# Ten graph steps and an attention layer on one core: dense groups finished one by one, node features in two copies, two VectorE operands moved to PSUM

## What is computed

```python
# part 1: ten steps over all edges and self loops
wn = w * inv_sqrt_out[s] * inv_sqrt_in[d]
def step(h, _):
    agg = segment_sum(h[s] * wn[:, None], d, num_segments=n)
    return (1.0 - ALPHA) * agg + ALPHA * feat_0
x = layernorm(x + ten_steps(x))
# part 2: edge attention, 8 heads of 8
score = Kh[src] * Qh[dst] * inv_sqrt_d * Eh            # Eh = edge_attr @ WE + bE
score = exp(clip(score.sum(-1), -5, 5))
wV = segment_sum(Vh[src] * score, dst, num_segments=n)
x = layernorm(x + wV)
```

## Time and profile before

| | |
|---|---|
| median of 3 runs | 13,851.04 us (13,825.7 to 13,856.41) |
| the profiled execution | 13,848.15 us, its span 13,846.3 us |
| busy | PE 73%, PEld 41%, DVE 41%, ACT 5%, POOL 64% |
| mean granted TensorE clock | 0.762 |
| DMA | 3,491.10 MB, mean 252 GB/s |

### The profile page before, as it was taken

How to read it: one execution, slowest core, us unless ns; L and a number is a source line. 1 busy time by engine, 2 the same in 40 slices (tenths; PEclk the granted TensorE clock), 3 DMA queues, 4 the chain that set the end, 5 groups by cost and what they waited for, 6 DMA issues and landing times.

```text
span 13846.3 us, 141202 instructions
## 1 busy us (share of the span) xinstructions
PE 10055.4 (73%) x48612; PEld 5626.1 (41%) x48612; DVE 5672.0 (41%) x18837; ACT 688.7 (5%) x2111; POOL 8874.1 (64%) x8640
## 2 busy tenths in 40 slices
PE   0199994877868778688686886867868676777667
PEld 0199991332323323233232332333323355555555
DVE  6188881342333333333333333332333434444444
ACT  0033330000000000000000000000000010000000
POOL 3678887666666666666666666666666646666555
PEclk5555556988979889799797997989979855555555
DMA  9963335988969879699696996979969643333333
GB/s 394 385 165 69 69 54 174 374 296 310 375 228 374 328 273 375 227 375 363 236 376 231 373 374 225 373 265 336 377 228 374 249 110 108 113 109 110 106 105 97
DMA packets 1722567, 3491.10 MB, mean 252 GB/s; under 512 B 820288, under 2 KB 836067, under 8 KB 1721846
## 3 DMA queue, kind: packets, MB, share of 16 engines
q1 hardware_dynamic: 1145060, 2896.46, 56.9%
q0 software_dynamic: 379456, 296.48, 9.9%
q10 hardware_dynamic: 197330, 289.05, 5.8%
HBM read 3177.87 MB, written 303.14 MB: 251 GB/s over the span
## 4 chain that ended last, share of the span: by engine, by line
PE 55%; issue 15%; DVE 14%; another core or an unknown queue 8%; ACTq 5%; POOL 1%; ACT 1%; DMA 1%; DVEq 0%; SPq 0%
PE banks L1977 39%; PE banks L1996 5%; ACTq L1495 5%; PE banks L1946 4%; DVE arena L1673 2%; DVE arena L1737 2%; PE banks L1947 2%; PE banks L2067 1%; PE banks L2043 1%; DVE arena L1851 1%; PE banks L1989 1%; POOL dense L1460 1%; ACT arena L1504 1%; DVE arena L1687 1%
## 5 line engine op out<-in xcount | busy, mean ns | idle before, releaser
L1471 POOL DMA_INDIRECT arena<-node_rows,src_idx x5880 | 5623.7, 956 | 3174.3 <-issue 1655.0
L1977 PE MATMUL banks<-arena,u_sb 128*64 128x512 f32 x19600 | 5680.6, 625 | 1481.9 <-issue 1248.3
L1977 PEld LDWEIGHTS banks<-arena,u_sb 128*64 128x64 f32 x19600 | 1765.4, 142 | 4722.1 <-issue 4699.1
L1752 DVE TENSOR_TENSOR arena<-banks,arena 128x104 f32<-128x104 f32 (+20 forms) x1030 | 259.5, 257 | 5356.9 <-remote 4728.4
L1486 POOL DMA_INDIRECT arena<-kv_rows,src_idx x1568 | 1581.8, 1009 | 1136.8 <-DVEq L1910 553.0
L1737 DVE TENSOR_SCALAR arena<-banks,rel,w_tab 128x128 f32<-128x128 f32 x5880 | 1963.5, 403 | 166.5 <-issue 100.5
L1460 POOL DMA_INDIRECT dense<-arena x980 | 1633.5, 1667 | 591.9 <-issue 246.6
L1946 PE MATMUL banks<-arena 128*128 128x98 f32 x3136 | 1140.8, 467 | 694.8 <-ACT arena L1504 694.8
L1996 PE MATMUL banks<-arena 128*64 128x128 f32 x11760 | 1039.2, 301 | 661.6 <-issue 425.7
L1996 PEld LDWEIGHTS banks<-arena 128*64 128x64 f32 x11760 | 794.3, 149 | 925.0 <-issue 721.3
L1946 PEld LDWEIGHTS banks<-arena 128*128 128x128 f32 x3136 | 848.9, 331 | 702.9 <-ACT arena L1504 702.8
(11 more groups left out here) (166 smaller groups left out, 5382.1 us busy)
## 6 DMA issues: line engine op xcount, KB each, us to landing
arena<-dense SPq DMA_DIRECT2D x4900, 512.0 KB
dense<-blank ACTq DMA_DIRECT2D x5, 50176.0 KB, 371.2
arena<-in_dst_dram SPq DMA_DIRECT2D x195, 512.0 KB
arena<-node_rows,src_idx POOLq DMA_INDIRECT x5880
arena<-in_edge_attr_dram SPq DMA_DIRECT2D x195, 256.0 KB
u_sb<-key_rows SPq DMA_DIRECT2D x25, 1280.0 KB
u_sb<-in_edge_weight_dram SPq DMA_DIRECT2D x25, 1280.0 KB
arena<-key_rows SPq DMA_DIRECT2D x24, 1280.0 KB
```

Source lines behind the costliest of these rows:

```text
L1471: gp.indirect_dma_start(out=rows_in[:, n % ROWS, s, :], out_offset=None, in_=node_rows[k % 2], in_offset=bass.IndirectOffsetOnAxis(ap=src_ ...
L1977: last = mm(banks[h * D:(h + 1) * D, g, :], u_sb[:, j * D:(j + 1) * D], ring[:, u % SLOTS, h * 512:(h + 1) * 512], start=m < GROUPS, stop= ...
```

## The change

Five things change together.

- The dense columns shrink from 5,120 to 4,992 (39 blocks): the last group has 896 columns, in the matrix, its clear, its loads and its matmuls.
- The units run group by group (`UNIT`): all 98 blocks for group 0, then group 1. They spread over 96 iterations. A group ends one iteration after its last unit, at 20, 39, 58, 77 and 96. Two PSUM banks take turns as accumulators.
- A step reads the features from one copy and writes the new ones to the other (`u_of`). The second copy takes 6,272 elements per partition: the ring falls from 18 to 15 slots and the gather buffers from 7 to 6.
- GpSimd waits for all of its adds to land before the steps.
- In the attention, the bases of the picks are copied into PSUM bank 7 for 24 iterations at a time (9 small copies), and ScalarE writes the exponentials into that bank. `pick` and the message product then have one operand in SBUF.

```diff
-DENSE_COLS = 5120
+DENSE_COLS = 4992
-SLOTS = 18
-ROWS = 7
-DENSE_ITERS = 84
+SLOTS = 15
+ROWS = 6
+DENSE_ITERS = 96
...
-    GROUP_AT = {DENSE_ITERS + 2 * g: g for g in range(GROUPS)}
+    LAST_BLOCKS = list(GROUP_BLOCKS[-1])
+    BLOCK_AT = [b for b in range(NB) if b not in LAST_BLOCKS] + LAST_BLOCKS
+    UNIT = [(g, j) for g in range(GROUPS) for j in BLOCK_AT]
     UNIT_AT = [n * DENSE_ITERS // UNITS for n in range(UNITS)]
-    BLOCK_AT = [(i + DENSE_BLOCKS) % NB for i in range(NB)]
+    GROUP_AT = {UNIT_AT[(g + 1) * NB - 1] + 1: g for g in range(GROUPS)}
...
-                if i >= DENSE_ITERS and not copied:
-                    act.wait_ge(unit_used, (k + 1) * UNITS)
-                    for g in range(GROUPS):
-                        nc.scalar.activation(dense_sum[:, g, :], banks[:, g, :], ACT.Copy).then_inc(sum_copied, 1)
-                    copied = True
+                for turn, g in GROUP_AT.items():
+                    if turn <= i and g == copied:
+                        nth = k * GROUPS + g
+                        act.wait_ge(unit_used, k * UNITS + (g + 1) * NB)
+                        if nth >= 2:
+                            act.wait_ge(sum_turned, nth - 1)
+                        nc.scalar.activation(dense_sum[:, nth % 2, :], banks[:, nth % 2, :], ACT.Copy).then_inc(sum_copied, 1)
+                        copied += 1
...
+        for s in range(STREAMS):
+            pool.wait_ge(added[s], 16 * ROUNDS)
...
-            return v.tensor_tensor(u3, part, o3, ALU.mult)
+            return v.tensor_tensor(new3, part, o3, ALU.mult)
...
-                nc.scalar.activation(score[:, a % 2, :, :], score[:, a % 2, :, :], ACT.Exp).then_inc(exp_made, 1)
+                nc.scalar.activation(exp_ps(a), score[:, a % 2, :, :], ACT.Exp).then_inc(exp_made, 1)
...
-            v.tensor_tensor(pick[:, a % 2, :].rearrange("p (t e) -> p t e", e=P), att_buf(a).rearrange("p (t e) -> p t e", e=P), base_p[:, t].unsqueeze(2).broadcast_to([P, 8, P]), ALU.is_equal).then_inc(pick_made, 1)
+            at = P + 4 * (a % (2 * BASE_TURNS))
+            if a % BASE_TURNS == 0:
+                upto = min(PAIRS, 4 * (a + BASE_TURNS))
+                edge(v.tensor_copy(banks[:, 7, at:at + upto - 4 * a], base_p[:, 4 * a:upto]))
+            base_ps = banks[:, 7, at:at + 4]
+            v.tensor_tensor(pick[:, a % 2, :].rearrange("p (r e) -> p r e", r=4), att_buf(a).rearrange("p (r e) -> p r e", r=4), base_ps.unsqueeze(2).broadcast_to([P, 4, 2 * P]), ALU.is_equal).then_inc(pick_made, 1)
```

More of the change, by code:

```diff
@@ L51 @@
 KV_BUFS = 4
+BASE_TURNS = 24
 ARENA = 29696
@@ L1048, in __init__ @@
         self.blank_set = sem("blank_set")
-        self.dense_cleared = [sem(f"dense_cleared{g}") for g in range(DENSE_COLS // GROUP)]
+        self.dense_cleared = [sem(f"dense_cleared{g}") for g in range(-(-DENSE_COLS // GROUP))]
         self.flag_ready = sem("flag_ready")
@@ L1080, in fast @@
     assert BASE[DENSE_TILES // 2 - 1] + P <= DENSE_COLS
-    GROUPS = DENSE_COLS // GROUP
+    GROUPS = -(-DENSE_COLS // GROUP)
+    WIDTH = [min(GROUP, DENSE_COLS - g * GROUP) for g in range(GROUPS)]
     ITERS = (TILES - DENSE_TILES) // TPI
@@ L1085, in fast @@
     DENSE_BLOCKS = DENSE_COLS // P
+    assert DENSE_BLOCKS * P == DENSE_COLS and WIDTH[-1] > 512
+    GROUP_BLOCKS = [range(8 * g, min(8 * g + 8, DENSE_BLOCKS)) for g in range(GROUPS)]
     FIRST_BLOCK = BASE[DENSE_TILES // 2] // P
     LATE = DENSE_BLOCKS - FIRST_BLOCK
+    assert GROUP_BLOCKS[-1][0] <= FIRST_BLOCK < DENSE_BLOCKS
     assert ITERS * TPI == TILES - DENSE_TILES and ITERS % 2 == 0 and DENSE_TILES % 2 == 0
@@ L1317, in fast @@
     for n, (kind, i, what) in enumerate(UPDATES):
-        for b in (what if kind == "tail" else range(what * 8, what * 8 + 8)):
+        for b in (what if kind == "tail" else GROUP_BLOCKS[what]):
             UPDATED_AT[b] = n
-            last_use = max(UNIT_AT[m] for m in range(UNITS) if BLOCK_AT[m // GROUPS] == b)
-            assert last_use <= i - (kind == "dense")
     assert len(UPDATED_AT) == NB
@@ L1474, in run_pool @@
         pool.wait_ge(steps_done, 1)
-        base_v = base_p.rearrange("p (r u) -> p r u", u=2)
         for at, n, first, slope in RUNS:
-            last = pool.iota(base_v[:, at:at + n, :], pattern=[[slope, n], [0, 2]], base=first, channel_multiplier=1, allow_small_or_imprecise_dtypes=True)
+            last = pool.iota(base_p[:, at:at + n], pattern=[[slope, n]], base=first, channel_multiplier=1, allow_small_or_imprecise_dtypes=True)
         last.then_inc(att_tables, 1)
@@ L1524, in run_act @@
                 act.wait_ge(updated, k * len(UPDATES) + n + 1)
-                j0, m = (what * 8, 8) if kind == "dense" else (what[0], len(what))
-                act.dma_start(to[j0 * P:(j0 + m) * P, :].rearrange("(j p) f -> p j f", p=P), u_sb[:, j0 * D:(j0 + m) * D].rearrange("p (j f) -> p j f", f=D)).then_inc(node_stored, 16)
+                blocks = GROUP_BLOCKS[what] if kind == "dense" else what
+                j0, m = blocks[0], len(blocks)
+                act.dma_start(to[j0 * P:(j0 + m) * P, :].rearrange("(j p) f -> p j f", p=P), u_new[:, j0 * D:(j0 + m) * D].rearrange("p (j f) -> p j f", f=D)).then_inc(node_stored, 16)
         kvq_at = 0
@@ L1757, in run_dve, with update @@
         step = Chain(dve, step_vec, fin.n)
-        def update(part, j0, m):
-            u3 = by_node(u_sb, j0, j0 + m)
+        def update(k, part, j0, m):
+            u3, new3 = by_node(u_of[k % 2], j0, j0 + m), by_node(u_of[(k + 1) % 2], j0, j0 + m)
             x3 = by_node(x_sb, j0, j0 + m)
@@ L1788, in run_dve @@
                     if len(late) < len(done):
-                        last = update(parts[:, len(late):len(done), :], done[len(late)], len(done) - len(late))
+                        last = update(k, parts[:, len(late):len(done), :], done[len(late)], len(done) - len(late))
                         last.then_inc(updated, 1)
@@ L1797, in run_dve @@
                     dve.wait_ge(sum_turned, k * GROUPS + g + 1)
-                    part = banks[:, g, :].rearrange("p (j f) -> p j f", f=D)
-                    if g * 8 + 8 > FIRST_BLOCK:
-                        b0 = FIRST_BLOCK - g * 8
-                        assert 0 <= b0 < 8 and g == GROUPS - 1
-                        step(v.tensor_tensor(part[:, b0:8, :], part[:, b0:8, :], carry[:, :, :], ALU.add))
-                    last = update(part, g * 8, 8)
+                    j0, m = GROUP_BLOCKS[g][0], len(GROUP_BLOCKS[g])
+                    part = banks[:, (k * GROUPS + g) % 2, 0:m * D].rearrange("p (j f) -> p j f", f=D)
+                    if g == GROUPS - 1:
+                        step(v.tensor_tensor(part[:, FIRST_BLOCK - j0:m, :], part[:, FIRST_BLOCK - j0:m, :], carry[:, :, :], ALU.add))
+                    last = update(k, part, j0, m)
                     last.then_inc(updated, 1)
-                    dve.wait_ge(updated, k * len(UPDATES) + UPDATED_AT[g * 8] + 1)
+                    dve.wait_ge(updated, k * len(UPDATES) + UPDATED_AT[j0] + 1)
                     dve.sem_inc(sum_read, 1)
```

43 lines of the change are left out of this document (25 added, 18 removed).

## The result

After takes 14,097.8 us (median of 4, 14,091.1 to 14,115.3), before 13,848.7 (4, 13,825.7 to 13,856.4): 1.0185 of before, 95% interval 1.0172 to 1.0198. That is 249 us slower, inside the range; the point, 13,866, was not it.

A forecast was written before the change was run, and what follows sets the result against it. Gathers and hand-offs, not DMA bandwidth, were taken to bound a step. From 13,848 us, steps +20 and +40, adds' landing +3, copies +2, attention -50, median +3 gave 13,866 us; range 13,620 to 14,150.

The forecast's parts named there:

- What bounds a step: In the steps, gathers and hand-offs between engines, not DMA bandwidth, set the pace: 8.77 us per window in two-window runs.
- The steps' terms, +20 and +40: Over ten steps: +20 us for a longer stream of gathers, +40 us for each step's last windows and closing.
- The hand-offs inside the stretch: Four group hand-offs per step among the units: taken as 0, with 31 us a step if TensorE's cover is gone.
- The DMA share: Sign in the steps' stretch: the share falls to about 0.87, from 0.99, if the forecast is right.
- The rival of transfers (8%): Transfers bound the steps' stretch: a step takes 806 us instead of 883, the kernel near 13,100 us; chance 8%.
- The attention, -50 with bounds of 0 and 82: Attention gathers lose 52 ns each with one pick operand in PSUM: 50 us saved, between 0 and 82.
- the rival "turn into gaps": The attention's delays stay or turn into gaps: +50 us, 13,916, within the forecast's own range; no separate chance given.
- The sum: Whole kernel: 13,848 + 20 + 40 + 3 + 2 - 50 = 13,863 us, and 3 more for the median: 13,866.
- the third rival: TensorE falls behind in the steps: four hand-offs cost 7.8 us each, +31 per step, 14,176 us; chance 18%.

The follow-up runs named there:

- quarters: After with attention in four 49-turn parts: bases and exponentials in SBUF; bases in PSUM; both in PSUM; both plus a clearing each turn; steps six to ten with clearings; 13,977.6 us.
- doses: After with GpSimd clearings of several sizes and frequencies per attention quarter, and two per window in steps six to ten; 13,938.5 us, 0.9963 of before, on a slowed chip.

## Why the prediction was right, and where it was wrong

- *What bounds a step: right for the profile it was made from.* Gathers and hand-offs, not bandwidth: the loads fell from 371 to 329 GB/s and a step stayed at 848.6 us of gathers. Breaks that add 51 us of work to a step (98 x 0.52) and leave it at 849 show the same, since an engine that is truly the bound can't do more work in the same time. What I took for the bound, "gathers with their gaps", is thus the pace of the other engines beside the gathers.
- *The steps' terms, +20 and +40: too large.* The stream stayed where it was, and the mean gap between steps went from 34.7 to 35.5 us where 4 more were forecast. Both together: 8,804.6 - 8,796.7 = +8 in place of +60. The hand-offs inside the stretch, taken as 0, show no cost: GpSimd's gaps at windows 20, 39, 58 and 77 stay at 2.5 to 2.7 us. The DMA share fell to 0.92, not 0.87.
- *The rival of transfers (8%): wrong here, right on a calm chip.* There, before's steps are bound by the loads, and after the change they aren't; what the spreading does of it and what the 2.5% fewer columns do wasn't told apart. The prediction had the mechanism and dismissed it by the earlier trace rows, which are true of a slowed chip alone.
- *The attention, -50 with bounds of 0 and 82: the step that failed.* The 52 ns a gather came off (1,009 to 956), so the reading of the stretched gathers was right, and calm chips pay it out in full. But here the stream got 241 us longer. "A delay that falls into a slow spell may only have shortened the next gap" was the right thought, and I let it reduce the gain to no less than zero; the rival "turn into gaps" likewise ended at +50. The runs show the term on the other side of zero: in `quarters`, moving the bases took 8.7 us off the gathers (391.35 to 382.66) and made 49 turns 57 us longer, GpSimd's waits for messages going from 128.4 to 219.7 us. Taken for all four quarters, 66.5 us times four are 266, beside the 241 of the two profiles. That a stretched gather works as a break in the run is my reading and isn't shown: one added break a turn does give 57 us back, but that adds 0.84 us to every turn, and the breaks of `doses` in every other turn, 21 us in all, bought nothing, where the first quarter's gathers are only 15.6 us longer in all than the third's.
- *The sum.* +8 (steps) + 241 (attention) - 6 around them = 243 between the profiled executions, 13,848 and 14,091. The forecast had +15. That the range held the time is luck: it reached up to 14,150 for the third rival, TensorE falling behind in the steps, and that didn't occur; the loss came from the attention, which was forecast as a gain.

## What to carry to other kernels

Where an engine's idle time grows with the length of another's uninterrupted run, its delays aren't only costs: before removing one, ask what catches up meanwhile, and bound the term on both sides of zero. A cheap way to learn whether an engine is the bound is to give it more work: on a calm chip 164 us of clearings cost 161 us, on a slowed one they gained. And a change of a few per cent has its sign only for the chip it was timed on: put variants into parts of one execution, and time the pair on several chips before keeping it.

## What the runs showed of the hardware

- The same kernel takes 12,330 or 13,840 to 13,990 us on one chip or another, each met once. TensorE's mean granted clock doesn't tell them apart (after had 0.783 in an execution of 14,091 us and 0.785 in one of 11,949, before 0.762 at 13,848 and 0.797 at 12,343), nor do the durations of single instructions (gathers 957 ns, picks 1,221 on both). What differs most is the time between instructions: "remote" waits and 0.82 us of "issue" beside runs of gathers, which calm chips don't show. The cause isn't known.
- On a slowed chip a clearing of 0.97 us by GpSimd, twice in eight gathers, removes GpSimd's waits for messages in the attention (3.1 us left in 98 turns). Two of 0.65 us leave 226.3 us of them, and one of 0.97 us in every sixteen gathers leaves all (212.1 us in 49 turns, 213.7 without).
- With the picks' bases in PSUM in place of SBUF, the gathers beside them are stretched less on either kind of chip (1,057 to 970 ns in the mean on a calm one, 998 to 976 on a slowed one).
- A clearing of 1,024 columns takes 970 ns and adds 840 to the stream: the gather behind it starts 0.17 us later and not 0.30.
